# Attention outputs on array quarters, kv products on column halves, and identity transposes in TensorE's waits

## The chip, the core and the metric

The kernel runs on one core of a Trainium2 chip. It is one launch; the metric is the device time of that launch in microseconds (us). TensorE does the matmuls and the transposes, VectorE and ScalarE read its results from eight PSUM banks, GpSimd works on SBUF alone, and SyncE issues the loads and stores. The engines run side by side and wait for each other through counters (semaphores).

## What is computed

```python
# tok: (4, 512, 256, 4) image tensor to (4, 512, 256) tokens; joined with the 512 text tokens to x: (4, 1024, 256)
h = einsum('bhid,oi,od->bho', x, weighted_sum, weight)

# attention layer on the normalised x: 16 heads of 64, linear attention over 1024 tokens
q, k = elu(x @ Wq) + 1, elu(x @ Wk) + 1;  v = x @ Wv;  g = sigmoid(x @ Wg + bg)
kv = einsum('bhnd,bhne->bhde', k, v);  k_sum = k.sum(-2)
z = 1 / clip(einsum('bhnd,bhd->bhn', q, k_sum), 1e-6)
out = einsum('bhnd,bhde->bhne', q * 64**-0.5, kv) * z[..., None] * g
x = x + out @ Wo

# then twice, on (2, 2048, 256): windowed attention (8 heads of 64, window 128, rotary, one window back),
# and a feed-forward of hidden size 682 with a GELU gate behind a layer norm
```

## The kernel before

The phases follow each other, each in a block whose end all engines wait for: the image tokens (`tok_phase`), the linear attention (`attention_phase`), and for each of two layers the windowed attention (`local_phase`) and the feed-forward (`mlp_phase`). Products that need more than one pass of precision are three matmuls on split operands (`matmul3`, lines 117 to 119; a record each). A plain float32 matmul leaves two records in the trace, a transpose (a matmul against the identity) one.

**Attention.** A batch has 1024 tokens, 8 tiles of 128. First the keys of all tiles are made and multiplied with the normalised x (`g_products`), which gives a matrix of 256 x 1024 in banks 2 to 5. ScalarE copies it out in four pieces (`take_g`, L516), and `kv_products` multiplies it with Wv (`attn_wv`, which carries one more column for the sum of the keys). Heads go in pairs: one matmul of a 128x128 stationary block with 129 moving columns makes the kv blocks of two heads, of which only the two diagonal 64x64 blocks are wanted; VectorE copies those, and the two key sums, out of banks 4, 5 and 3 into `kv`, whose other blocks are zero (`take_kv`, 12 copies, L660 and L661). The 4 stages u of a batch take two tiles each: queries (`queries`, four parts f), gates (`gates`, two halves a tile), head outputs (`outputs`), and, one stage later, the output transposes and products with Wo (`out_transposes`, `out_products`) and the residual.

`outputs` multiplies a pair's q (128 channels x 128 tokens, stationary) with its 128x130 block of `kv`: 128 columns of outputs and two of denominators. A tile's eight pairs go in groups of 3, 3 and 2, which use banks 4 and 5 in turn. VectorE answers each group in `gated` with four operations: the clipped denominator (L641), its reciprocal (L643), the multiply (L645) and the gate (L649). A bank is free when the group's fourth operation is done. TensorE's order is written out in `batch`: between the groups of a stage stand gate halves, each six matmuls of 512 columns, and the output products.

**Local attention.** `step(n, ...)` on each engine handles tile n's projections (banks 0 and 1), the turn of q and k and the scores of tile n-1, and probabilities and values of tile n-2. The turn (`turned_t`) waits for GpSimd's rotated q and k (L1075), the scores use array quarters already: 64 rows and 64 columns of the array each, with 64, 128 or 192 moving columns (L1391); the values use column halves (L1415). Four steps at the head and three at the end are written out, the others loop.

**Feed-forward.** `group` works on four tiles; its first group's normalised input is transposed at the end of the local phase (L1492).

SyncE issues all loads in one queue in the order of the code: in the first phase the image tiles (L192), between them the attention weights (L197).

## Time and profile before

| | us |
|---|---|
| median of 3 runs (lowest, highest) | 1915.9 (1913.65, 1916.27) |
| the profiled execution | 1916.24 |
| its span, first to last instruction | 1914.2 |
| TensorE busy in the span | 1841.3 (96%) |
| VectorE busy | 1512.0 (79%) |
| ScalarE busy | 1102.2 (58%) |
| GpSimd busy | 432.2 (23%) |
| image tokens | 0 to 62 |
| attention | 62 to 634 |
| local attention and feed-forward, layer 0 | 634 to 1068, 1068 to 1273 |
| layer 1 | 1273 to 1706, 1706 to 1914 |

The page gives for each engine the time in which at least one instruction ran. A matmul's record lasts longer than the array is taken by it (they are pipelined), so the pace is read from one start to the next. The granted clock is a share of 2.4 GHz: 1.00 is the higher of TensorE's two levels, 0.50 (1.2 GHz) the lower. Its mean over the span is 0.986.

### The profile page before, as it was taken

The numbers are of one execution on the slowest core, as the hardware profiler recorded it, in microseconds if no ns is written. First come the engines' busy times: TensorE is split into PE (matmuls) and PEld (weight loads), VectorE is DVE, ScalarE is ACT, GpSimd is POOL, SyncE is SP. The second block draws the span as 40 slices with busy tenths as digits, with TensorE's granted clock in tenths as the row PEclk, the third lists the DMA queues.
The fourth block names the chain that finished last, engine by engine and source line by source line (L and its number), as shares of the span: only waits on it lengthen the run. The fifth ranks groups of instructions, "written<-read, shape, count | busy, mean of one in ns | idle before, by whom it ended". The sixth has DMA issues, their size and how long they took to land. (4 is left out here: it accounts for less than half of the span.)

```text
span 1914.2 us, 44588 instructions
## 1 busy us (share of the span) xinstructions
PE 1841.3 (96%) x15388; PEld 1612.0 (84%) x15388; DVE 1512.0 (79%) x4715; ACT 1102.2 (58%) x2551; POOL 432.2 (23%) x319
## 2 busy tenths in 40 slices
PE   8899999999999799999999899989999999989998
PEld 8789889889889588888888788867888888868887
DVE  6888878878778688888888677768888888877777
ACT  4433433433433388888888444437888888853333
POOL 0000000000000244454444000014554545411111
PEclk9999999999999799999999999998999999999999
DMA  9100000000010100000000200010000000000002
GB/s 344 49 1 1 1 1 1 1 1 1 1 69 1 51 6 5 5 4 5 5 5 11 87 12 11 11 45 4 6 4 5 5 5 5 4 23 12 11 11 93
DMA packets 44983, 44.51 MB, mean 23 GB/s; under 512 B 8359, under 2 KB 39387, under 8 KB 44894
## 3 DMA queue, kind: packets, MB, share of 16 engines
q1 hardware_dynamic: 44894, 43.33, 6.9%
q8 instruction: 55, 0.90, 0.2%
q14 instruction: 34, 0.28, 0.0%
HBM read 34.93 MB, written 8.39 MB: 23 GB/s over the span
## 5 line engine op out<-in xcount | busy, mean ns | idle before, releaser
L1117 ACT ACTIVATE l_probs<-l_probs,l_negmax 128x256 f32<-128x256 f32 x512 | 253.1, 496 | 83.3 <-DVE l_negmax L1227 83.3
L1075 POOL TENSOR_TENSOR l_t<-l_t,l_rnorm 128x512 f32<-128x512 f32 x128 | 131.0, 1044 | 295.3 <-DVE l_rnorm L1244 295.3
L1070 POOL TENSOR_TENSOR l_t<-l_t,l_t 128x1024 f32<-128x1024 f32 x64 | 153.2, 2393 | 129.0 <-DVE l_t L1279 129.0
L117 PE MATMUL ps<-local_w_hi,l_xT 128*128 128x512 f32 x384 | 167.7, 437 | 9.0 <-DVE l_t L1279 3.3
L118 PE MATMUL ps<-local_w_lo,l_xT 128*128 128x512 f32 x384 | 153.7, 400 | 0.0
L486 ACT ACTIVATE attn_exp<-ps 128x512 f32<-128x512 f32 x128 | 76.4, 599 | 133.2 <-PE ps L119 133.2
L119 PE MATMUL ps<-local_w_hi,l_xT 128*128 128x512 f32 x384 | 153.1, 399 | 0.0
L1405 PE MATMUL ps<-ident,l_probs 128*128 128x128 f32 x1024 | 145.7, 279 | 1.6 <-ACT l_probs L1117 1.4
L117 PE MATMUL ps<-m_hnT_hi,ffn_w_hi 128*128 128x512 f32 (+1 forms) x352 | 142.4, 405 | 4.3 <-PEq L1017 4.3
L118 PE MATMUL ps<-m_hnT_lo,ffn_w_hi 128*128 128x512 f32 (+1 forms) x352 | 139.6, 396 | 0.0
L119 PE MATMUL ps<-m_hnT_hi,ffn_w_lo 128*128 128x512 f32 (+1 forms) x352 | 139.6, 396 | 0.0
L1123 ACT ACTIVATE l_probsT<-ps 128x512 f32<-128x512 f32 x256 | 134.3, 648 | 0.0
L1050 POOL MEMSET l_xT<- 128x520 f32 x2 | 1.1, 531 | 571.7 <-POOLq L450 569.8
L1405 PEld LDWEIGHTS ps<-ident,l_probs 128*128 128x128 f32 x1024 | 113.4, 140 | 17.5 <-issue 12.4
L1415 PE MATMUL ps<-l_probsT,l_v 128*64 128x128 f32 x2048 | 125.9, 276 | 0.7 <-DVE x L1195 0.7
L1415 PEld LDWEIGHTS ps<-l_probsT,l_v 128*64 128x64 f32 x2048 | 110.5, 137 | 12.1 <-issue 10.0
L1622 ACT ACTIVATE m_gelu<-ps,ffn_b 128x512 f32<-128x512 f32 x80 | 55.1, 688 | 109.5 <-PE ps L119 109.5
L1274 DVE TENSOR_TENSOR l_t<-ps,rope_c 128x1024 f32<-128x1024 f32 x64 | 78.4, 1225 | 40.7 <-PE ps L1399 38.9
L117 PE MATMUL ps<-attn_w_hi,attn_xT_hi 128*128 128x512 f32 x256 | 106.1, 414 | 3.8 <-PEq L185 2.1
L1609 ACT ACTIVATE m_u_hi<-m_u 128x512 fp32r<-128x512 f32 x80 | 50.5, 632 | 99.1 <-DVE m_u L1683 99.1
L1227 DVE CUSTOM_DVE_ANT_0 l_probs<-ps,mask_even 128x256 f32<-128x256 f32 x256 | 107.0, 419 | 0.0
L1227 DVE CUSTOM_DVE_ANT_0 l_probs<-ps,mask_odd 128x256 f32<-128x256 f32 x256 | 106.5, 419 | 0.1
(252 smaller groups left out, 5774.5 us busy)
## 6 DMA issues: line engine op xcount, KB each, us to landing
tok_x<-x SPq DMA_DIRECT2D x16, 512.0 KB, 7.9
m_shifted<-shifted SPq DMA_DIRECT2D x20, 256.0 KB, 2.8
shifted<-x SPq DMA_DIRECT2D x64, 64.0 KB, 1.5
out<-x SPq DMA_DIRECT2D x8, 512.0 KB, 4.2
ffn_w_raw<-ffn_w SPq DMA_DIRECT2D x6, 640.0 KB
local_w_raw<-ffn_wqkv SPq DMA_DIRECT2D x4, 768.0 KB, 5.6
tok_base<-attn_base SPq DMA_DIRECT2D x4, 512.0 KB, 8.6
h<-txt SPq DMA_DIRECT2D x4, 512.0 KB, 8.4
```

The source lines that it names most:

```text
L117: nc.tensor.matmul(out, wh, mh, start=start, stop=False, skip_group_check=True)
L118: nc.tensor.matmul(out, wh, ml, start=False, stop=False, skip_group_check=True)
L119: return nc.tensor.matmul(out, wl, mh, start=False, stop=stop, skip_group_check=True)
L486: nc.scalar.activation(ex[:, at % 2], ps[:, at % 2], ACT.Exp).then_inc(s.attn_exp.sem, 1)
L1070: nc.gpsimd.tensor_tensor(t1[:], t1[:], t2[:], ALU.add).then_inc(s.summed.sem, 1)
L1075: nc.gpsimd.tensor_tensor(v, v, rn[:, a * LH:(a + 1) * LH].unsqueeze(2).to_broadcast([P, LH, DH]), ALU.mult).then_inc(s.rotated.sem, 1)
L1117: last = nc.scalar.activation(v, v, ACT.Exp, bias=nb[:, h:h + 1], scale=-1.0, accum_out=rsum[:, h:h + 1])
L1123: nc.scalar.activation(pt[:, pair], ps[:, PT[pair]], ACT.Copy).then_inc(s.p_done.sem, 1)
L1227: last = nc.vector.tensor_tensor_reduce(pm[:, pair, e * 2 * P:(e + 1) * 2 * P], ps[:, bank, at:at + 2 * P], mask[:], -8.0, -LOWEST, ALU.ad ...
L1274: nc.vector.tensor_tensor(t1[:].rearrange("p a (h d) -> p a h d", d=DH), q, cw, ALU.mult)
L1405: last = nc.tensor.transpose(ps[:, PT[pair], k * P:(k + 1) * P], pm[:, pair, k * P:(k + 1) * P], K.ident[:])
L1415: last = nc.tensor.matmul(ps[e * DH:(e + 1) * DH, OT, pair * P:(pair + 1) * P], vv[:, w, h * DH:(h + 1) * DH], pt[:, pair, (2 * e + w) * P ...
```

## The change

**Outputs.** Each of the eight pairs of a tile now takes four matmuls: for each half of the tokens and each head of the pair, 64 rows by 64 columns of the array with 65 moving columns (64 outputs and the denominator). Head e writes bank 4 + e. `kv` has no zero blocks any more. A tile's pairs go in two groups of four, and each group uses both banks; a bank is free when the group's multiply, now counted by itself, is done. The second group of a stage's second tile is gated one stage later.

**kv products.** Each head has its own matmul per half of the contraction: 128 rows by 64 columns of the array, 65 moving columns. The first four pairs wait for the first two pieces of `take_g`, the others for all four. `take_kv` is two copies of 128x260. `attn_wv` is laid out in 16 blocks of 65 columns, so its loads go in rows of 64 elements.

**Transposes of the identity.** `keep_warm` issues `count` transposes of the identity into a bank; nobody reads them. They stand at the end of the image tokens (8), of the attention (10), at several places of each local phase (4, 10, 6, 20, 18, 8 around its first steps, 20, 8, 8 in its last three, 8 behind them), at each feed-forward's start (8) and after the first feed-forward (10).

```diff
+def keep_warm(nc, K, bank, count):
+
+    for _ in range(count):
+        nc.tensor.transpose(K.ps[:, bank, 0:P], K.ident[:], K.ident[:])
...
-    VC = P + 1
-    OC = P + 2
-    GROUPS = ((0, 3), (3, 6), (6, 8))
-    KV_BANKS = (4, 5, 3)
+    OC = DH + 1
+    PG = PAIRS // 2
...
             def gated(b, n, *groups):
                 for g in groups:
...
+                    done = OB * b + 4 * n + 2 * g
+                    dve.wait_ge(*s.attn_o_full.after(FB * b + 2 * n + g + 1))
+                    out = ps[:, 4:6, 0:PG * OC].rearrange("p e (m c) -> p m e c", c=OC)
+                    heads = (lambda v: v.rearrange("p (m e) -> p m e", e=2).unsqueeze(3))
+
+                    chain(nc.vector.tensor_scalar(heads(zd[:]), out[:, :, :, DH:OC], 1e-6, 2.0 * DH ** 0.5, ALU.max, ALU.mult))
+                    chain(nc.vector.reciprocal(z[:], zd[:]))
+                    nc.vector.tensor_tensor(o1[:, g].rearrange("p (m e d) -> p m e d", e=2, d=DH), out[:, :, :, 0:DH],
+                                            heads(z[:]).to_broadcast([P, PG, 2, DH]), ALU.mult).then_inc(s.attn_o.sem, 1)
+                    dve.wait_ge(*s.attn_o.after(done + 1))
...
             def take_kv(b):
...
+                for g in range(2):
+                    done = nc.vector.tensor_copy(kv[:, g * PG:(g + 1) * PG, :],
+                                                 ps[:, 4 + g, 0:PG * OC].rearrange("p (m c) -> p m c", c=OC))
...
             def kv_products(b):
-                pe.wait_ge(*s.attn_gt.after(4 * b + 4))
...
+                for g in range(2):
+                    pe.wait_ge(*s.attn_gt.after(4 * b + 2 * g + 2))
+                    for m in range(g * PG, (g + 1) * PG):
                         for c in range(KC):
...
+                            for e in range(2):
+                                h = 2 * m + e
+                                last = nc.tensor.matmul(ps[e * DH:(e + 1) * DH, 4 + g, m % PG * OC:(m % PG + 1) * OC],
+                                                        gt[:, c, h * DH:(h + 1) * DH], wv[:, c, h, :],
+                                                        start=(c == 0), stop=(c == KC - 1))
...
+            def outputs(b, u, which, g):
                 n = 2 * u + which
...
+                pe.wait_ge(*s.attn_o.after(OB * b + 4 * n + 2 * g - 1))
+                for m in range(g * PG, (g + 1) * PG):
+                    for half in range(2):
+                        tokens = slice(half * DH, (half + 1) * DH)
+                        for e in range(2):
+                            r = slice(e * DH, (e + 1) * DH)
+                            last = nc.tensor.matmul(ps[tokens, 4 + e, m % PG * OC:(m % PG + 1) * OC],
+                                                    qt[r, m, which * P + half * DH:which * P + (half + 1) * DH], kv[r, m, :],
+                                                    start=True, stop=True)
+                last.then_inc(s.attn_o_full.sem, 1)
...
                 if b:
                     wait(pe, s.masked, 4 * (n - 1))
+                    if second:
+                        keep_warm(nc, K, OT, 20)
+                    if drain(n, 0):
+                        wait(pe, s.turned, n)
+                        keep_warm(nc, K, QK, 20)
                     turned_t(n - 1, 0)
...
+                if second:
+                    keep_warm(nc, K, OT, 18)
                 if b:
                     wait(pe, s.qk_done, 2 * n)
...
+            keep_warm(nc, K, OT, 4)
             x_t(0, 0)
+            keep_warm(nc, K, OT, 10)
             schedule(pe, step)
+            keep_warm(nc, K, V, 8)
...
+            keep_warm(nc, K, 4, 8)
             group(0, 0, False)
...
-            ("attn_wv", [P, KC, PAIRS, P + 1], F32),
+            ("attn_wv", [P, KC, 2 * PAIRS, DH + 1], F32),
```

TensorE, first stage of the first batch, around the first tile's head outputs (L848 before, L853 now; the rows between are a gate half). Before:

```order
L848 MATMUL ps<-attn_kv,attn_qT 128x130 x6
L117 MATMUL ps<-attn_w_hi,attn_xT_hi 128x512
L118 MATMUL ps<-attn_w_lo,attn_xT_hi 128x512
L119 MATMUL ps<-attn_w_hi,attn_xT_lo 128x512
L117 MATMUL ps<-attn_w_hi,attn_xT_hi 128x512
L118 MATMUL ps<-attn_w_lo,attn_xT_hi 128x512
L119 MATMUL ps<-attn_w_hi,attn_xT_lo 128x512
L848 MATMUL ps<-attn_kv,attn_qT 128x130 x2
```

Now:

```order
L853 MATMUL ps<-attn_kv,attn_qT 64x65 x16
L117 MATMUL ps<-attn_w_hi,attn_xT_hi 128x512
L118 MATMUL ps<-attn_w_lo,attn_xT_hi 128x512
L119 MATMUL ps<-attn_w_hi,attn_xT_lo 128x512
L117 MATMUL ps<-attn_w_hi,attn_xT_hi 128x512
L118 MATMUL ps<-attn_w_lo,attn_xT_hi 128x512
L119 MATMUL ps<-attn_w_hi,attn_xT_lo 128x512
L853 MATMUL ps<-attn_kv,attn_qT 64x65 x16
```

Six matmuls, then two, on both sides of the gate half have become sixteen and sixteen.

VectorE at the same place, its answer to the outputs, behind the last operation of the norm (L133, now L139). Before:

```order
L133 SCALAR_TENSOR_TENSOR attn_rstd<-attn_tmp,attn_rstd 128x8
L641 TENSOR_SCALAR attn_den<-ps 128x6
L643 RECIPROCAL attn_z<-attn_den 128x6
L645 TENSOR_TENSOR attn_o_1032<-ps,attn_z 128x384
L649 SCALAR_TENSOR_TENSOR attn_out<-attn_tanh,attn_o_1032 128x384
L641 TENSOR_SCALAR attn_den<-ps 128x6
```

Now:

```order
L139 SCALAR_TENSOR_TENSOR attn_rstd<-attn_tmp,attn_rstd 128x8
L646 TENSOR_SCALAR attn_den<-ps 128x8
L647 RECIPROCAL attn_z<-attn_den 128x8
L648 TENSOR_TENSOR attn_o_1040<-ps,attn_z 128x512
L654 SCALAR_TENSOR_TENSOR attn_out<-attn_tanh,attn_o_1040 128x512
L646 TENSOR_SCALAR attn_den<-ps 128x8
```

The operations are the same four; they cover 512 elements instead of 384, and a tile has two such groups instead of three.

TensorE in the second step of a local phase, from the last projection to the scores (L1403 is the turn of q and k, L1370 the turn of the next x, L1395 the scores). Before:

```order
L119 MATMUL ps<-local_w_hi,l_xT 128x512
L1399 MATMUL ps<-ident,l_t_8239 128x128 x8
L1366 MATMUL ps<-ident,l_x 128x128 x2
L1391 MATMUL ps<-l_kT,l_qT 64x128 x4
```

Now:

```order
L119 MATMUL ps<-local_w_hi,l_xT 128x512
L125 MATMUL ps<-ident 128x128 x20
L1403 MATMUL ps<-ident,l_t_8728 128x128 x8
L1370 MATMUL ps<-ident,l_x 128x128 x2
L125 MATMUL ps<-ident 128x128 x18
L1395 MATMUL ps<-l_kT,l_qT 64x128 x4
```

Twenty transposes of the identity stand ahead of the turn, eighteen ahead of the scores.

## Rows read from the trace of the kernel before

**Rows 1.** Windows: us; busy (instructions) per engine, PEclk (granted clock), DMA share, GB/s

```profile
62.00:620.60 558.60, 549.63 (x3588) 495.28 (x3588) 441.29 (x1093) 216.92 (x402) 1.09 (x2) 1.00 0.02 7
637.00:676.00 39.00, 30.52 (x229) 23.99 (x230) 29.73 (x109) 19.60 (x52) 12.83 (x9) 0.79 0.19 58
```

**Rows 2.** Timeline of TensorE, one stage's outputs: start, us, engine, line, operands, count

```profile
192.97 1.51 PE L848 MATMUL ps<-attn_kv,attn_qT 128*128 128x130 f32 x12
194.23 0.47 PE L117 MATMUL ps<-attn_w_hi,attn_xT_hi 128*128 128x512 f32 x1
...
201.04 0.83 PE L848 MATMUL ps<-attn_kv,attn_qT 128*128 128x130 f32 x6
```

**Rows 3.** Timeline of TensorE, local scores (array quarters) and values (column halves), from several windows

```profile
683.03 0.27 PE L1424 MATMUL ps<-ident,l_spread 128*128 128x128 f32 x1
683.23 0.51 PE L1391 MATMUL ps<-l_kT,l_qT 64*64 64x128 f32 x12
683.23 0.56 PE L1391 MATMUL ps<-l_kT,l_qT 64*64 64x128 f32 x16
683.23 1.57 PE L1391 MATMUL ps<-l_kT,l_qT 64*64 64x128 f32 x64
684.73 1.97 PE L1415 MATMUL ps<-l_probsT,l_v 128*64 128x128 f32 x32
```

**Rows 4.** Timeline of VectorE in a stage: a 512-element feature, denominator, multiply

```profile
188.66 0.69 DVE L598 SCALAR_TENSOR_TENSOR attn_qT<-ps,attn_exp 128x512 f32<-128x512 f32 x1
...
193.84 0.17 DVE L641 TENSOR_SCALAR attn_den<-ps 128x6 f32<-128x6 f32 x1 [0.46 <-PE ps L848]
...
194.27 0.56 DVE L645 TENSOR_TENSOR attn_o<-ps,attn_z 128x384 f32<-128x384 f32 x1
```

**Rows 5.** Timelines of ScalarE and TensorE around kv; group of VectorE's larger copies

```profile
255.91 2.06 ACT L516 ACTIVATE attn_out<-ps 128x512 f32<-128x512 f32 x4 [2.15 <-PE ps L119]
258.02 3.84 PE L823 MATMUL ps<-attn_wv,attn_out 128*128 128x129 f32 x32 [0.72 <-ACT attn_out L516]
261.62 0.36 PE L117 MATMUL ps<-attn_xT_hi,attn_w_hi 128*128 128x256 f32 x1
L660 DVE COPY attn_kv<-ps 64x192 f32<-64x192 f32 (+1 forms) x24 | 8.0, 333 | 2.4 <-PE ps L823 2.1
```

**Rows 6.** Timeline of TensorE, end of attention and second and third local step

```profile
622.90 1.94 PE L947 MATMUL ps<-ident,attn_out 128*128 128x128 f32 x8 [2.24 <-DVE attn_oT_lo L759]
...
650.99 2.12 PE L1399 MATMUL ps<-ident,l_t 128*128 128x128 f32 x8 [2.75 <-POOL l_t L1075]
...
661.48 0.63 PE L118 MATMUL ps<-local_w_lo,l_xT 128*128 128x512 f32 x1
661.91 0.63 PE L119 MATMUL ps<-local_w_hi,l_xT 128*128 128x512 f32 x1
...
664.42 0.60 PE L1399 MATMUL ps<-ident,l_t 128*128 128x128 f32 x4
```

**Rows 7.** Timeline of TensorE, start of layer 0's feed-forward

```profile
1068.77 0.47 PE L117 MATMUL ps<-m_hnT_hi,ffn_w_hi 128*128 128x512 f32 x1 [2.14 <-PEq L1017]
...
1073.64 0.39 PE L119 MATMUL ps<-m_hnT_hi,ffn_w_lo 128*128 128x512 f32 x1
1073.87 0.40 PE L117 MATMUL ps<-m_hnT_hi,ffn_w_hi 128*128 128x512 f32 x1
```

**Rows 8.** Timelines of GpSimd and TensorE, first step of layer 0's drain

```profile
1042.97 2.04 POOL L1075 TENSOR_TENSOR l_t<-l_t,l_rnorm 128x512 f32<-128x512 f32 x2 [4.72 <-DVE l_rnorm L1244]
1044.16 0.63 PE L1399 MATMUL ps<-ident,l_t 128*128 128x128 f32 x4 [2.59 <-POOL l_t L1075]
```

**Rows 9.** Window of TensorE with transposes alone: busy (records), granted clock, DMA

```profile
1042.60:1046.10 3.50, 1.94 (x17) 1.00 0.01 2
```

**Rows 10.** Timeline of SyncE's issues in the first phase

```profile
15.43 3.27 SPq L197 DMA_DIRECT2D attn_wv<-attn_Wv  x2
...
26.48 0.93 SPq L197 DMA_DIRECT2D attn_w_raw<-attn_Wq  x2
```

More of the change, by code:

```diff
@@ L838, in queries @@
                 last.then_inc(s.attn_a_full.sem, 1)
-            def outputs(b, u, which, *groups):
+            def outputs(b, u, which, g):
                 n = 2 * u + which
@@ L843, in outputs @@
                 pe.wait_ge(*s.attn_kv.after(b + 1))
-                for g in groups:
-                    m0, m1 = GROUPS[g]
-                    pe.wait_ge(*s.attn_o.room(OB * b + 3 * n + g, 2))
-                    for m in range(m0, m1):
-                        last = nc.tensor.matmul(ps[:, 4 + (3 * n + g) % 2, (m - m0) * OC:(m - m0 + 1) * OC],
-                                                qt[:, m, which * P:(which + 1) * P], kv[:, m, :],
-                                                start=True, stop=True)
-                    last.then_inc(s.attn_o_full.sem, 1)
+                pe.wait_ge(*s.attn_o.after(OB * b + 4 * n + 2 * g - 1))
[8 more added lines that the diff above has]
+                last.then_inc(s.attn_o_full.sem, 1)
             def out_transposes(b, last, u, which):
```

84 lines of the change are left out of this document (36 added, 48 removed).

## The prediction

> **What bounds the kernel now.** I read first the stages by windows, then the timelines of TensorE and of the engines that it waits for. In the attention stage TensorE is busy 549.6 of 558.6 us and VectorE 441.3 [rows 1]: what is taken off TensorE there comes off the time, as long as VectorE's answers come in time. At the head of each local layer the picture is another: in 39 us TensorE works 30.5, at a mean granted clock of 0.79 [rows 1]. There a chain over ScalarE, VectorE and GpSimd sets the pace, and TensorE stands at the lower of its two levels (1.2 GHz) for part of its work. The profiled execution took 1916.2 us, its span is 1914.2; the median of the runs is 1915.9, so the sum is made against 1916.2 and needs no shift worth naming.
>
> **Head outputs.** Before, 16 records of 130 columns make a tile (two per matmul): 12 of them from 192.97 to 194.23, 0.105 each, and six in 0.83 us, of which the last takes 0.28, 0.11 each [rows 2]. That is some 3.46 us for the 32 records of a stage (two tiles). Now 64 records of 65 columns make a tile, on four array quarters in turn. The trace has that form in the local scores. Going from 12 to 16 records, four records of 64 columns, lengthens the run by 0.05 us [rows 3], and the whole run, half of it fours of 128 columns, takes 64 records from 683.23 to 684.73 [rows 3]. I take 0.055 for a four: eight fours are 0.44. Around a group the array changes its form: 683.03 to 683.23 is 0.20 where such records stand 0.11 apart, and the step out costs as much again, so a group is 0.44 + 0.2 = 0.64, say 0.66. Four groups are 2.64, 0.82 less per stage. Twelve stages (three of each of four batches) give **9.8 us**; the fourth is in the batch heads below. Bounds: without the change of form 0.46 a group, 13 us more for 64 groups; with fours at twice 0.055, 28 us less.
>
> **Can VectorE keep up?** The two output banks now hold one group at a time: the next group waits for the multiply of the one before. Behind that wait stand, in TensorE's order, everything else of the stage. A group's answer is tensor_scalar, reciprocal and multiply. From 193.84 the multiply begins 0.43 later; over 512 elements it takes about 0.69, as the 512-element feature does [rows 4]. With the hand-over that is 1.25 us; between the two groups lie the six projections of a gate half, 6 x 0.23 = 1.4 (the two records of this form at the higher level, [rows 7]). It fits, by a tenth. The other pairs are parted by the same, by 12 projections of 256 columns, or by 2.8 us of output products. I count no wait in a stage. VectorE's own work falls too (two groups of four operations a tile instead of three), which keeps it from becoming late in its turn; the late group, now half a tile, delays the next features by 0.6, which nobody waits for.
>
> **Batch heads.** The kv products take 258.02 to 261.62 and stand 0.72 idle before, for the last of ScalarE's four copies, 2.06 us together [rows 5]. Now half of them need two copies only, so that idle goes. 64 records of 65 columns on column halves come in pairs; the 128-column pairs of the values take 32 records in 1.97 us [rows 3], so I take half of it for a pair, 0.057, and 2.0 for all. TensorE is 2.3 us ahead. VectorE takes kv over in two copies (0.85) instead of 12, whose larger six are 8.0 us in 24 records over four batches [rows 5], with the small ones 2.5 a batch. Behind them stand two features and ten small operations before the first gate, so VectorE, 2.2 ahead, now makes TensorE wait some 0.5 for the first multiply. With 0.8 for the outputs of the stage a head gives 2.9; in the first batch VectorE is held by the subtraction for Wo's low part ahead of it, and I take 2.3. Sum **11.0 us**. If column halves do not overlap at 65 columns, 6 of these are lost.
>
> **End of attention.** TensorE waits 2.24 us for VectorE there [rows 6]; one group of four operations in place of two saves 0.9 of the chain. The clock was low right after: the eight transposes took (1.94 - 0.35) / 7 = 0.23 each, twice 0.11, and the 20 products behind them, half as wide as those of [rows 7], lose some 0.1 each. About 2.4 of that lies on the path. The wait is now shorter, and whether the clock falls again I leave even: 1.2. Together **2.1**.
>
> **The turned identity.** 264 transposes are added, 118 for each layer with its feed-forward start. One is one record of 128 columns, 0.11 us; 29 us in all, of which what fits in a wait is free. What they bring is clock, and only where TensorE is on the chain. Step by step through layer 0: 10 behind the last product (1.1 us) lie beside two sums and statistics of VectorE; 4 and 10 lie in the waits around the first turn. 20 (2.2 us) fit in the 2.75 before 650.99 [rows 6]; 18 end before the scores. At the higher level the turn of q and k ends 0.4 earlier (its second half waits for GpSimd), and the 12 projections from 659.64, nine of them at 0.43 each, end 2.4 us earlier (0.43 from one start to the next at the lower level, 0.23 at the higher, [rows 6, 7]), but then GpSimd's rotated halves are the later ones, which gives 1.0 at 664.42 [rows 6]; of all that I keep 0.9 beside 0.4 from the first projections, since VectorE has its late statistics to finish. **1.3** for layer 0. Layer 1 has no late statistics: its first projections, at the lower level too, would go from 0.43 to 0.23, and 1.4 us pass through; **2.4**. Feed-forward start: eight transposes stand ahead of the first product, 0.9 lost, since the first product, at 1068.77, waits only for the barrier; eight products behind it, at the lower level, go from 0.43 to 0.23, 1.6 won [rows 7]. **1.4** for two. Drain: 20 transposes begin only when the last mask is done, just before GpSimd begins at 1042.97, so they end at about 1045.0, while q's half was turned from 1044.16 [rows 8]. That is a delay of 0.85 on a chain in which all wait, twice: **minus 1.7**. The rest (8 each) fits.
>
> Do transposes hold the clock? From 1042.6 to 1046.1 TensorE did nothing but transposes, busy 1.94 of 3.5 us, and the granted clock stayed 1.00 [rows 9]. The page "TensorE: Matmul & The Clock Gate" of the Trainium skill, in Part 4 (PE-mode transpose), says that the full clock does not engage for transposes, which don't count as busy the same way; by it the added work would buy nothing. The row speaks against it, though for holding a clock, not for raising it.
>
> **Loads.** Wv lands in chunks of 64 elements instead of 128. Issuing its two halves took SyncE 3.27 us where Wq, in long rows, took 0.93 [rows 10], and image tiles queue behind it on SyncE while the first stage waits for them. Bounds 0 (queues absorb it) and 2.3 (as much again); near the lower, as the following issue waits for room anyway: **minus 0.7**.
>
> **Sum.** 9.8 + 11.0 + 2.1 + 1.3 + 2.4 + 1.4 - 1.7 - 0.7 = 25.6: 1916.2 - 25.6 = **1890.6 us**.
>
> **Rivals.** *The warm work doesn't hold the clock.* The ramps then stay at 1.2 GHz and a transpose costs about twice 0.11, as those at 622.90 did [rows 6]: 20 would end 1.7 after their wait, 18 and the next 8 some 3 later. No gain of 6.3, and about 3 lost in each layer: 1890.6 + 6.3 + 6 = 1903. For it: the transposes at 650.99 ran at the lower level and did not raise it. Against it: [rows 9]. Chance 0.12. *Output banks.* If the chain to the multiply takes 0.5 more than I add up, two of four groups a stage wait, 16 us in all: 1907. Chance 0.06. *Column halves don't overlap* in the kv products: 1897, chance 0.08. *Cheap quarters*: no cost for the change of form, and all cold stretches gone: 13 + 3 less, 1875; with half of it 1882; chance 0.1. *Slower:* only two of the four quarters run at once, as the column halves of the values do. Then a record is 0.03 us (half of 1.97 / 32), a group 0.96 + 0.2 = 1.16, 64 groups cost 32 us more: 1923. It turns slower once a group costs 0.40 more than my 0.66. What speaks against it is the 0.05 for four. Chance 0.03. The same page, in Part 1, gives a floor of about 25 ns from one start to the next however few the columns; by it a group of 32 would be 1.0 us and the time about 1912. Four records more in 0.05 us [rows 3] speak against it. Chance 0.01.
>
> **How the numbers follow.** The forecast case has 0.6. Its own range is 1884 to 1897. The range for 8 in 10 takes in the kv case and the clock case: 1881 to 1904; outside stay the bank case, the two-quarter case and the floor, and half of the cheap case. A measurement of this kernel tells about 0.2% (4 us) from no change. Faster by more needs under 1912: 0.94; within 0.02; slower 0.04.
>
> **What would show it.** Groups of 32 records of 64x65 in about 0.66 us from start to next, with no idle before them but once a batch; kv in 2.0 us without the 0.72 before it; attention from 558.6 to about 538; a granted clock of 1.00 from 637 on in the local ramps, and 0.85 more before the turn in the drain. Wrong would be: idle before most output groups, released by the multiply (bank case); groups over 1 us; a clock at 0.5 under the added transposes; a later end of the first stage, released by image tiles.

## The result, and the profile after the change

The changed kernel took **1905.3 us** (median of four runs, 1903.2 to 1906.5) beside 1916.1 of the kernel before on the same chip: a ratio of 0.9947, 95% interval 0.9934 to 0.9960. It is faster, by 10.8 us or 0.5%. The forecast was 1890.6 with a range of 1881 to 1904, so the time lies outside, and less than half of the forecast gain came. The profiled execution of the changed kernel took 1904.3 us, 12.0 less than that of before; the ledger below is made against these two.

The windows of the changed kernel, with the columns of [rows 1]:

```profile
62.00:620.00 558.00, 549.11 (x5306) 474.70 (x5305) 424.06 (x937) 218.54 (x404) 0.21 (x1) 1.00 0.03 7
620.00:637.00 17.00, 13.27 (x73) 10.88 (x72) 9.82 (x31) 3.87 (x7) 3.90 (x7) 0.84 0.47 142
637.00:676.00 39.00, 35.34 (x392) 30.09 (x392) 29.64 (x109) 25.32 (x66) 15.99 (x12) 0.98 0.01 3
627.00:666.00 39.00, 32.18 (x279) 26.70 (x278) 29.61 (x109) 19.56 (x52) 12.82 (x9) 0.91 0.18 56
```

Against [rows 1]: in 637 to 676 the granted clock is 0.98 instead of 0.79. But the same work now stands some 10 us earlier, and in 627 to 666 the clock is 0.91; that is the figure to set beside 0.79. The attention stage is where the forecast and the trace part. TensorE's last products of attention come 11 us earlier, not 22.

**A ledger by the same record.** Both timelines hold the same fp32 products in the same order, only other records stand between them. So the start of one product before and after says how far the changed kernel is ahead at that place. Each line is one such record, starts in us. Within a stage the lead swings by some 0.5, since the old first group holds three pairs and the new one four, so batches are compared at the same place of a stage: the last product ahead of a stage's first group. The head of a batch is all that lies up to its second stage's outputs, the kv products and the first stage's outputs with it.

```
place                              before    after    ahead
end of the first stage              64.09    65.01    -0.93
batch 0, at stage 2's outputs      147.51   146.69     0.82
batch 0, behind its stages         246.09   244.79     1.30
batch 1, at stage 2's outputs      286.80   283.17     3.63
batch 1, behind its stages         386.94   382.88     4.06
batch 2, at stage 2's outputs      426.05   419.67     6.38
batch 2, behind its stages         528.70   521.87     6.83
batch 3, at stage 2's outputs      565.71   556.67     9.04
batch 3, at stage 4's outputs      610.13   600.95     9.18
last output product's run          630.41   619.43    10.98
layer 0, first turn                650.99   642.41     8.58
layer 0, third step                671.23   661.12    10.11
layer 0, before the drain         1040.09  1029.96    10.13
layer 0, in the drain             1046.80  1037.47     9.33
feed-forward start, layer 0       1075.04  1064.83    10.21
layer 1, first product            1275.12  1265.12    10.00
layer 1, third step               1315.16  1302.89    12.27
layer 1, in the drain             1694.80  1683.43    11.37
feed-forward start, layer 1       1716.85  1704.59    12.26
last transposes' end              1906.39  1894.46    11.93
```

The heads give 1.8, 2.3, 2.3 and 2.2, together 8.6. The stages behind them give 0.5, 0.4, 0.5 and 0.1, together 1.5 for eleven stages, 0.14 each, where 0.82 was forecast; the twelfth stands with the end of attention. That end gives 1.8, layer 0's ramp loses 0.9, layer 1's gives 2.3, each drain loses 0.8 and each feed-forward start gives 0.9 at first.

**A group of head outputs** in the changed kernel's timeline of TensorE, with the product ahead of it and the ones behind:

```profile
193.63 0.40 PE L118 MATMUL ps<-attn_w_lo,attn_xT_hi 128*128 128x512 f32 x1
193.87 0.39 PE L119 MATMUL ps<-attn_w_hi,attn_xT_lo 128*128 128x512 f32 x1
194.19 0.70 PE L853 MATMUL ps<-attn_kv,attn_qT 64*64 64x65 f32 x32
194.81 0.50 PE L117 MATMUL ps<-attn_w_hi,attn_xT_hi 128*128 128x512 f32 x1
195.15 0.39 PE L118 MATMUL ps<-attn_w_lo,attn_xT_hi 128*128 128x512 f32 x1
```

and the products ahead of the first record of [rows 2], before the change:

```profile
192.51 0.39 PE L118 MATMUL ps<-attn_w_lo,attn_xT_hi 128*128 128x512 f32 x1
192.74 0.40 PE L119 MATMUL ps<-attn_w_hi,attn_xT_lo 128*128 128x512 f32 x1
```

The group is 194.19 to 194.81, 0.62 (0.63 in the median of 54), where the forecast had 0.66. But the last product ahead of it holds TensorE from 193.87 to 194.19, 0.32; before, from 192.74 to 192.97, 0.23. And the first product behind it takes 0.34 to the next (194.81 to 195.15); that behind the old group, at 194.23, took 0.31. A part of the price of the form stands on its neighbours.

**kv and the rest of a head** (TensorE, batch 0):

```profile
117.37 2.09 PE L826 MATMUL ps<-attn_wv,attn_out 128*64 128x65 f32 x64
119.39 0.38 PE L117 MATMUL ps<-attn_xT_hi,attn_w_hi 128*128 128x256 f32 x1
...
124.42 0.47 PE L117 MATMUL ps<-attn_w_hi,attn_xT_hi 128*128 128x512 f32 x1 [1.90 <-issue]
```

2.02 for 64 records, where [rows 5] had 3.60 for 32, with no idle time ahead. In batch 0 TensorE then stands 1.90 before the first gate (1.29 before the change): it waits for kv, which VectorE takes over only behind the subtraction for Wo's low part. That 0.6 is lost again there.

**End of attention and layer 0's ramp**, windows (same columns) and timelines of TensorE and VectorE:

```profile
611.23:614.64 3.41, 1.19 (x9) 0.84 (x8) 2.53 (x5) 1.79 (x4) 0.00 (x0) 1.00 0.00 0
614.64:618.05 3.41, 3.02 (x14) 3.05 (x15) 1.50 (x4) 0.05 (x1) 0.00 (x0) 0.50 0.00 0
628.29:631.71 3.42, 1.06 (x5) 0.53 (x3) 2.87 (x17) 2.09 (x4) 0.00 (x0) 1.00 0.96 362
631.71:638.53 6.82, 5.96 (x17) 4.89 (x18) 6.52 (x15) 0.00 (x0) 2.36 (x1) 0.50 0.44 124
```

```profile
612.90 1.16 PE L950 MATMUL ps<-ident,attn_out 128*128 128x128 f32 x8 [1.64 <-DVE attn_oT_lo L760]
...
628.27 0.17 DVE L157 TENSOR_REDUCE l_rstd<-h_stats 128x8 f32<-128x16 f32 x1 [2.25 <-DMA mask_odd<-mask_prev]
...
632.57 0.80 PE L117 MATMUL ps<-local_w_hi,l_xT 128*128 128x512 f32 x1 [3.21 <-DVE l_xT L1191]
```

The wait at the end of attention is 1.64 instead of 2.24 [rows 6], and the clock still falls behind it, in 614.64 to 618.05, after a stretch in which TensorE worked 1.19 of 3.41 us. Then something that the forecast didn't have: VectorE's late statistics wait 2.25 for the masks' DMA, which they don't read. TensorE stands idle for 3.21, until the l_xT that VectorE makes behind the statistics is there, and the clock falls for the 6.8 us in which it has to catch up. The masks landed late too, from the table of DMA issues (last column: us from issue to landing; 1.8 before):

```profile
mask_odd<-mask_prev SPq DMA_DIRECT2D x1, 64.0 KB, 3.0
```

**Drain, feed-forward start, loads** (GpSimd, TensorE, SyncE's issues), which answer to [rows 8], [rows 7] and [rows 10]:

```profile
1032.84 2.05 POOL L1079 TENSOR_TENSOR l_t<-l_t,l_rnorm 128x512 f32<-128x512 f32 x2 [4.72 <-DVE l_rnorm L1248]
...
1032.71 2.37 PE L125 MATMUL ps<-ident 128*128 128x128 f32 x20 [1.28 <-issue]
1034.92 0.49 PE L1403 MATMUL ps<-ident,l_t 128*128 128x128 f32 x3
...
1059.31 1.06 PE L125 MATMUL ps<-ident 128*128 128x128 f32 x8 [1.12 <-PEq L1021]
1060.12 0.48 PE L117 MATMUL ps<-m_hnT_hi,ffn_w_hi 128*128 128x512 f32 x1
...
15.56 7.44 SPq L203 DMA_DIRECT2D attn_wv<-attn_Wv  x2
```

From the start of the rotation to the first turned record it is 2.08 (1032.84 to 1034.92) where it was 1.19 in [rows 8]: 0.89 for the 20 transposes. The two issues for Wv take SyncE 7.44 instead of 3.27.

### The profile page after: what moved, and what is told of

Read it like the earlier page. It is cut to its first block and busy times, and to the rows that moved or that the text cites. A ratio compares the mean times of both kernels' runs of the same rounds, so it can differ in the third digit from the quotient of the medians.

```text
span 1902.2 us, 48258 instructions
## 1 busy us (share of the span) xinstructions
PE 1848.1 (97%) x17316; PEld 1601.8 (84%) x17316; DVE 1488.2 (78%) x4547; ACT 1102.7 (58%) x2551; POOL 431.6 (23%) x318
## 5 line engine op out<-in xcount | busy, mean ns | idle before, releaser
L117 PE MATMUL ps<-local_w_hi,l_xT 128*128 128x512 f32 x384 | 165.7, 432 | 6.4 <-DVE l_xT L1191 3.2
L119 PE MATMUL ps<-local_w_hi,l_xT 128*128 128x512 f32 x384 | 151.3, 394 | 0.0
L117 PE MATMUL ps<-m_hnT_hi,ffn_w_hi 128*128 128x512 f32 (+1 forms) x352 | 141.0, 401 | 0.0
L119 PE MATMUL ps<-m_hnT_hi,ffn_w_lo 128*128 128x512 f32 (+1 forms) x352 | 138.3, 393 | 0.0
L117 PE MATMUL ps<-attn_w_hi,attn_xT_hi 128*128 128x512 f32 x256 | 106.8, 417 | 3.5 <-issue 1.9
```

Source lines behind the costliest of these rows:

```text
L117: nc.tensor.matmul(out, wh, mh, start=start, stop=False, skip_group_check=True)
L119: return nc.tensor.matmul(out, wl, mh, start=False, stop=stop, skip_group_check=True)
```

## The experiments

The theory after reading the trace (A): the quarters cost as forecast inside a group, and give most of the gain back on the records around it and through a shift of Wo in memory; ramps and drains are, but for layer 0's ramp, nearly as forecast. Its rivals: the added transposes eat the gain; or the outputs are worth what was forecast, and it is lost elsewhere. The changed kernel is the starting point of each unless said.

### Which half of the change brings what

**forms_only**: `keep_warm` issues nothing, and the drain's wait ahead of it is gone.

> The changed kernel without any of its added transposes: head outputs on quarters and kv on column halves stay. Theory A (the trace of the changed kernel read by TensorE's starts): the groups of 32 records take 0.63 us, as forecast, but the projection ahead of a group takes 0.32 instead of 0.23 and the step out of a group 0.15 instead of 0.03, so the stages gain nothing like 0.82 each; attention is worth 11 us less 1 for the loads, and the added transposes bring next to nothing in sum: 1905 to 1907. Theory B (the prediction's sum): the forms are worth 22 us and the transposes lose most of it again: 1894.

1909.1 us (ratio 0.9963, 0.9951 to 0.9975): 7.1 better than before. That is 2 above A's range, and B's 1894 is out. What A missed is in its trace: the first stage ended 2.6 late instead of 0.9, and in batch 0's head, behind the idle 1.9 us, the clock fell:

```profile
126.00:129.40 3.40, 3.31 (x8) 2.61 (x9) 3.12 (x11) 0.55 (x1) 0.00 (x0) 0.55 0.00 0
```

In the profile of the changed kernel the same products ran at 1.00 behind the same idle time. The difference is 1.6 us; what decides over it isn't shown.

This run also shows the clock rising under transposes. In the first drain step TensorE has only the kernel's own transposes (of q and k, and of the probabilities) from 1037.32 to 1041.56; in the first window below it is busy throughout at 0.50, and from its end on the clock is 1.00:

```profile
1037.72:1041.13 3.41, 3.41 (x19) 3.41 (x17) 3.24 (x13) 1.94 (x5) 1.90 (x2) 0.50 0.00 0
1041.13:1044.54 3.41, 3.41 (x25) 3.15 (x24) 2.54 (x16) 1.71 (x4) 0.00 (x0) 1.00 0.00 0
```

**warm_only**: the kernel before with the transposes.

> The kernel before with all of the added transposes and nothing else of the change. Theory A: layer 1's ramp gains 2.4, the two drains lose 0.8 each and the two feed-forward starts gain 0.7 each, layer 0's ramp, where TensorE only comes to the late statistics' wait earlier and stands idle longer, gives between -0.9 and +0.5: 1912.5 to 1915. Theory B: if the transposes are what lost the gain, 1925 or more.

1912.3 (0.9980, 0.9971 to 0.9988): 3.8 better than before. With forms_only the two make 10.9, the whole change 10.8: they add. By the ledger it gains 0.3 in layer 0's ramp, 2.2 in layer 1's, and next to nothing over a drain and the feed-forward start behind it. The profiled execution (1914.1) is only 2.1 better than that of before; it is the second slowest of twelve. The transposes did not lose the gain.

**kv_halves_only**: head outputs as before.

```diff
-                            last = nc.tensor.matmul(ps[tokens, 4 + e, m % PG * OC:(m % PG + 1) * OC],
...
+                        last = nc.tensor.matmul(ps[:, 4 + (3 * n + g) % 2, (m - m0) * OC:(m - m0 + 1) * OC],
+                                                qt[:, m, which * P:(which + 1) * P], kv[:, m, :],
```

> The changed kernel with its kv products on column halves and its added transposes, but with the head outputs as before (full array, two heads a record of 130 columns, groups of 3, 3 and 2 pairs, kv block-diagonal and filled by four copies). Theory A: quarters are worth nothing in the stages, only about 1 at the end of attention; 1905 to 1908, level with the changed kernel within 2. Theory B: quarters are worth 0.82 in each of 16 stages and the loss is elsewhere: 1918.

1913.7 (0.9988, 0.9979 to 0.9997). Between the two: the quarters are worth 8.4, neither 0 nor 13. Theory A was wrong in saying that they bring nothing in the stages: beside the kernel before, this kernel **loses** 0.6 to 0.9 us in every three stages although its outputs are the old ones. So a part of the loss in the stages is not the quarters'. It stands on the products with Wo: 24 records of L117 to L119, in the timelines of before (the first two rows), of the changed kernel (the next two) the first and the last of one such run:

```profile
442.51 0.28 PE L117 MATMUL ps<-attn_wo_hi,attn_oT_hi 128*128 128x256 f32 x1
...
445.14 0.28 PE L119 MATMUL ps<-attn_wo_hi,attn_oT_lo 128*128 128x256 f32 x1
```

```profile
435.86 0.28 PE L117 MATMUL ps<-attn_wo_hi,attn_oT_hi 128*128 128x256 f32 x1
...
438.61 0.28 PE L119 MATMUL ps<-attn_wo_hi,attn_oT_lo 128*128 128x256 f32 x1
```

2.63 from first to last before, 2.75 after. Over the runs of the attention stage they are 2.62, 2.79 or 2.72 before (11, 11 and 6 of them) and 2.76 or 2.86 after (17 and 11): 2.71 and 2.80 on average.

### What the form costs, and whose

**row_halves**: one record for 128 tokens on each row half, 16 in place of 32.

```diff
-                    for half in range(2):
-                        tokens = slice(half * DH, (half + 1) * DH)
...
+                        last = nc.tensor.matmul(ps[:, 4 + e, m % PG * OC:(m % PG + 1) * OC],
+                                                qt[r, m, which * P:(which + 1) * P], kv[r, m, :], start=True, stop=True)
```

> The changed kernel with its head outputs on two row halves instead of four quarters: 16 records of 65 columns a group, each for 128 tokens, in place of 32. Same banks, same waits, same order. Theory A1: the price stands on the change between fp32 projections at full array and a divided array, whatever the division: entry 0.32, exit 0.15, inside 0.47 as before; 1905 within 1.5. Theory A2: the price goes with the columns' division, and with the tokens whole the entry is 0.23 and the exit 0.03: 64 groups by 0.2, 1892. Theory C: two row halves don't run at once, then a pair costs 0.11 and a group 0.4 more: 1931.

1928.1 (1.0061, 1.0047 to 1.0074; the median of six, of which one took 5052 us; without that one it is 1927.7), some 22 slower than with quarters:

```profile
202.25 0.40 PE L119 MATMUL ps<-attn_w_hi,attn_xT_lo 128*128 128x512 f32 x1
202.57 1.11 PE L851 MATMUL ps<-attn_kv,attn_qT 64*128 64x65 f32 x16
203.61 0.39 PE L117 MATMUL ps<-attn_wo_hi,attn_oT_hi 128*128 128x256 f32 x1
```

Two answers. The step in is 0.32 again (202.25 to 202.57): A1 holds for a division by rows alone as for quarters. Column halves pay it too: in the changed kernel the product ahead of kv takes 0.21 (255.72 to 255.93), where its like stand 0.12 apart.

```profile
255.72 0.28 PE L119 MATMUL ps<-attn_xT_hi,attn_w_lo 128*128 128x256 f32 x1
255.93 2.09 PE L826 MATMUL ps<-attn_wv,attn_out 128*64 128x65 f32 x64
```

So all three divisions of this kernel cost 0.09 on the record ahead. The second answer: the group is 1.04 for half the records, so the row halves do not run at once here, a record is some 0.06 by itself, as long as a four of quarters. That is C's mechanism, and 22 of its 26 us.

**groups_twice**: each group issued twice in a row, `for m in [*range(g * PG, (g + 1) * PG)] * 2`.

> The changed kernel with each group of head outputs issued twice in a row, 64 records in place of 32, the same result written again. Theory A (a four of quarters costs 0.0587 and the rest of a group's price, some 0.4 in all, is entering and leaving the form): 64 groups by 8 x 0.0587 = 0.47, 30 us more, 1935, and the group in the trace 1.10 from its first start to the next instruction. Theory B (the price is by the record, 0.9 for 32 with what stands on its neighbours): 64 x 0.9 = 58 us more, 1963.

1932.2 (1.0091, 1.0075 to 1.0106), some 27 more:

```profile
201.73 0.40 PE L119 MATMUL ps<-attn_w_hi,attn_xT_lo 128*128 128x512 f32 x1
202.06 1.16 PE L853 MATMUL ps<-attn_kv,attn_qT 64*64 64x65 f32 x64
203.15 0.50 PE L117 MATMUL ps<-attn_w_hi,attn_xT_hi 128*128 128x512 f32 x1
```

64 records take 1.09 where 32 took 0.63: 0.466 for eight fours, 0.058 each, and 64 groups of it are 30. By the ledger each stage of batch 1 loses 1.8, four times 0.466, but the head of the batch only 1.3: there a part of it lies in waits. The step in is the 0.32 or 0.33 of the single group. A holds: the rest of a group's cost, 0.16 inside the group's span and 0.11 on its neighbours, is paid per entry, however many records follow. The page "TensorEngine Tiling (Array Packing)" of the Trainium skill, under Key Properties, says that changing the tiling mode drains TensorE. No run shows the drain itself, but the rows show a price of that kind: 0.09 more ahead, the first four 0.11 where later ones stand 0.058 apart, and 0.15 from the last record to the next product, where the old group had 0.03.

### Wo's place

**wo_aligned**: 64 unused bytes a partition.

```diff
-            ("attn_wv", [P, KC, 2 * PAIRS, DH + 1], F32),
+            ("attn_wv", [P, KC, 2 * PAIRS, DH + 1], F32), ("attn_pad", [P, 16], F32),
```

> The changed kernel with 64 bytes of unused space a partition behind Wv, so that Wo's two parts lie 128 bytes from where they lay before the change instead of 64. In the trace of the kernel before, output products (attn_wo read as the moving side) start 116 ns apart on average, in that of the changed kernel 120, over some 660 records, and the same 120 stands where only kv was changed. Theory A: the place in memory makes that difference; 2.5 us less than the changed kernel, 1903. Theory B: it comes from what else reads and writes at that time; 0, 1905.

1902.3 (0.9923, 0.9909 to 0.9937), 3.0 better by the medians. By the ledger against the changed kernel it gains 0.2 to 0.5 in each batch, 1.5 in all, and the runs of 24 records are 2.71 and 2.81 instead of 2.76 and 2.86. So the place counts, with half the size that theory A gave it; the other half of the 3.0 isn't traced: in the profiled execution, 1.9 better in all, the clock did not fall at the end of attention (1.3 gained) and did in batch 0's head (1.6 lost). Why the place matters isn't shown. The 64 bytes move Wo on to 128 bytes behind its old place, not back to it, kv moves with it, and half of the difference to before is left (2.75 on average, beside 2.71 before and 2.80 in the changed kernel).

**full_outputs_aligned**: kv_halves_only with the same 64 bytes, which put Wo where it is in wo_aligned (its old place is 128 bytes in front of that).

> Head outputs as before on the full array, kv products on column halves, added transposes, and the 64 bytes behind Wv that put Wo back in its old place. Beside the changed kernel with the same 64 bytes (1902.3) it gives what the quarters alone are worth. By the prediction's sum 13 us for 64 groups and 0.9 at the end: 1916. By the trace (0.73 a stage inside the groups, less 0.35 for the entries and 0.1 for the first projection behind): 16 x 0.3 + 1.5 = 6 us: 1908.5.

1911.3 (0.9978, 0.9968 to 0.9987). Quarters alone are worth 1911.3 - 1902.3 = 9.0 by the medians: above the 6 from the trace, below the 13.9 of the forecast. But not all of that is the price of the groups. Beside wo_aligned, place by place: 3.4 in eleven stages, which is 0.3 a stage where 0.82 was forecast; 1.0 in each head, since with whole outputs VectorE fills kv by four copies and TensorE waits longer for it (2.88 in batch 0 and 0.63 in batch 1, where wo_aligned has 1.90 and nothing); 3.2 at the end of attention, where the clock fell in this profile and not in that of wo_aligned; and 1.0 lost again behind. In batch 3 its stages take what they took before: 47.995 us from the record at 550.34 on, 47.923 before.

### The other terms

**no_wait_gates**: `pe.wait_ge(*s.attn_kv.after(b + 1))` ahead of `gates(b, 0)` is left out.

> The changed kernel without the wait for kv ahead of the first gate of a batch (it was there since the kv products used gate bank 3, which they no longer do; the head outputs behind it keep theirs). Theory A: in the first batch TensorE stands idle 1.9 us there, of which the six projections that now move in front take most, until VectorE's features are the later ones: 1.0 to 1.9 less, and in some executions 1.6 more, where that gap makes the clock fall; 1903.5. Theory B: the features of VectorE are what ends the wait anyway and nothing moves: 1905.

1904.6 (0.9933, 0.9919 to 0.9946). In batch 0 the kernel is 2.0 ahead of its own earlier lag at the gate and has lost it again behind the second group of outputs. That is B: TensorE waits 1.21 for a feature and 0.87 for the multiply instead.

Its profile shows something else: the clock fell neither at the end of attention nor in the ramp (1.00 from 611 to 640, 0.82 there in the changed kernel), and it gained 2.4 there with the same code and nearly the same waits (1.64 and 3.31 idle, 1.64 and 3.21 in the changed kernel). What decides over such a fall isn't shown.

**drain_light**: no 20 transposes in the drain; the 8 at the feed-forward's start moved to the end of the local layer.

> The changed kernel without the 20 transposes ahead of the turn in the drain, and with the 8 ahead of the first feed-forward product moved to the end of the local layer (18 in place of 8 there). Theory A (each is in the path): 0.8 and 0.7 come back in each of two layers, the clock stays up: 3.0 less, 1902.3. Theory B: without the 8 at the start of the feed-forward the clock falls there as before the change and costs 1.6 each: 1.6 - 1.8 = no gain, 1905.5.

1905.5 (0.9939, 0.9925 to 0.9953), no difference. By the ledger the drain gains its 0.8 twice, as A has it. The 18 transposes at the layer's end cost 0.5, since the feed-forward starts only when TensorE is through them, and the 8 at the start had cost 0.7, so that moving them gains 0.1 in layer 0. In layer 1 the clock falls behind it, and of the lead 2.6 is lost, 1.6 of it on products at the lower level:

```profile
1712.96:1716.37 3.41, 3.41 (x10) 2.64 (x9) 2.73 (x5) 1.26 (x2) 0.00 (x0) 0.50 0.26 76
```

**ramp0**: 14 transposes in the last wait of attention, and the masks' wait behind the statistics.

```diff
+            keep_warm(nc, K, 0, 14)
             pe.wait_ge(*s.attn_o.after(OB * B))
...
-            if layer == 0:
-                dve.wait_ge(*s.const_in.after(16 * len(K.tables(0) + K.signs + K.masks)))
             late_stats()
+            if layer == 0:
+                dve.wait_ge(*s.const_in.after(16 * len(K.tables(0) + K.signs + K.masks)))
```

> The changed kernel with two edits around the end of attention: 14 transposes of the identity in the wait for the last head outputs, and VectorE's wait for the masks moved behind the late statistics, which don't read them. Theory A: the clock's fall there costs the last output products 1.3 us; the masks land 2.25 us after VectorE has nothing else to do, and TensorE's 3.6 us of idle behind the second projection, which makes the clock fall for the next 6.8 us, is mostly that wait: 1.3 + 2 to 3, 1901.5. Theory B: GpSimd's rotation is the later one in the ramp whatever is done before it, so that only the first edit counts: 1904.

1903.9 (0.9934, 0.9920 to 0.9947). By the ledger it is 1.3 ahead of the changed kernel behind the first edit and 4.4 behind both, at a clock of 1.00 throughout:

```profile
611.00:640.00 29.00, 25.26 (x176) 21.49 (x175) 17.61 (x52) 8.40 (x15) 6.25 (x9) 1.00 0.27 83
```

A, in the trace. Of the 4.4 the profiled execution keeps 2.3 (1901.9 beside 1904.3), since a fall of the clock at 1073 in the feed-forward took 1.9 back; the medians differ by 1.4.

**loads_split**: Wv's second half issued behind the next image tile.

> The changed kernel with Wv's two halves issued behind two image tiles instead of both behind one. In the traces of kernels with Wv in 64-element chunks the first stage ended 0.7 to 2.9 us later than before the change (mean 1.7 of eight), with Wv as before 0 and 0.3. Theory A: the two issues in a row (7.4 us of SyncE) are what the image tiles wait for, and split they fit between them: 1 to 1.7 less, 1904. Theory B: the transfers themselves, in four times as many small pieces, are what delays the tiles: no difference, 1905.3.

1906.0 (0.9947, 0.9934 to 0.9961). B: no difference, the first stage ended 3.5 late in its profile. Wv's two issues took SyncE 0.70 and 0.56 now, but the image tile between them 4.98. (A piece of 64 elements is half of the old one, so there are twice as many, not four times.)

**all_but_wo_lo** and **all_edits**: the padding, the ramp's edits, the drain without its 20, Wv's halves apart and 10 transposes in the first feed-forward group's wait; all_edits also moves the subtraction for Wo's low part behind `gated(b, 1, 0)`.

> The changed kernel with what the runs so far point to, together: Wo aligned as before (-2.5), no 20 transposes in the drain (-1.6), 14 transposes in the last wait of attention and the masks' wait behind the late statistics (-2.5 to -4), Wv's halves apart (-1), and 10 transposes in the first feed-forward group's wait for its normalised tile, where the clock fell in one of the runs. Theory A (the edits lie on different stretches and add): 1897. Theory B (one late arrival gives way to the next): 1901.

> The same, and in the first batch VectorE's subtraction for Wo's low part (2.29 us) is taken out of the way of kv and stands behind the first three groups of head outputs. Theory A: TensorE's 1.9 us of idle there goes, and with it the fall of the clock seen in two of the runs: 1.9 less than the kernel without this edit on average, 1895. Theory B: features and the outputs' multiply then are late by as much in the stage behind: no difference.

1899.4 (0.9913, 0.9900 to 0.9927) and 1897.7 (0.9910, 0.9895 to 0.9926). Not all of it adds: the first profile has falls of the clock in batch 0's head (1.5) and in the drain (1.5), where the 20 transposes no longer stand; in the drain it fell in wv_staged too, and not in all_edits or drain_light. Behind the moved subtraction TensorE gains 2.1 and loses 1.7 again, to features that are later by as much (waits of 0.49 and 1.14 at 136 and 139): B, but for the clock, which never falls in that profile while TensorE has work:

```profile
core 0: 1894.7 us, clock 0.999
```

**wv_staged**: Wv in long rows, where loads_split had only spread its pieces; its two issues stand together again.

```diff
-        K.attn_raw = [[(K.attn_wv[:, c, :, 0:DH], K.attn_wraw[:, k - (k > 1), c])[k != 1] for c in range(KC)]
+        (wv_raw,), _ = mem.place(K.attn_rest - PAIRS * D * 4, mem.norm, ("attn_wv_raw", [P, KC, INNER], F32))
+        K.attn_raw = [[(wv_raw[:, c], K.attn_wraw[:, k - (k > 1), c])[k != 1] for c in range(KC)] for k in range(4)]
...
+                out = K.attn_wv[:, c, :, 0:DH]
-            done = nc.vector.tensor_tensor(raw, raw, row, ALU.subtract)
+            done = nc.vector.tensor_tensor(out, raw, row, ALU.subtract)
```

> All edits of the best kernel so far, but Wv is loaded in its long rows (as Wq is) into the place that Wo's raw weights take later, and VectorE's subtraction of the base row, which ran in place, writes it into the layout of 64 elements and a gap. No instruction more. Theory A (the small pieces of Wv's transfer are what delays image tiles): the first stage ends 1 to 2.5 us earlier, 1896. Theory B (the tiles are late for another reason): no difference, 1897.7.

**1894.9** (0.9895, 0.9880 to 0.9911), the best kernel of the study, 20.4 below the kernel before (1915.3 beside it) and 10.4 below the changed one. SyncE issues both halves in 0.91:

```profile
16.46 0.91 SPq L203 DMA_DIRECT2D attn_wv_raw<-attn_Wv  x2
```

and its first stage ends with that of before (within 0.05 at 78 and 103 us). A: the small pieces were the loss, 2.8 us by the medians. With the pieces the first stage's delay was 0.8 to 3.5 us, by the kernel; one profile of each was taken.

## Why the prediction was wrong, step by step

- **Head outputs, 9.8 forecast, 1.5 in the ledger (0.14 a stage for 0.82). This is the step that failed.** It was "around a group the array changes its form, ... so a group is 0.44 + 0.2". The group itself came out as said: 0.058 for a four (0.055), 0.63 a group (0.66). What stands around it was left out. All starts of TensorE from 275.40 to 376.06 (before), the last three stages of batch 1 and the products behind them, summed by what stands ahead and what follows, give in us:

```
                                        before   after
inside the groups (81, 372 steps)         9.08    5.76    -3.32
step into a group (12)                    2.46    3.52    +1.06
step out of a group (12)                  0.66    1.76    +1.10
transposes of normalised x, and out (16)  1.59    1.51    -0.08
product to product (489)                 78.52   79.89    +1.37
all                                                       +0.13
```

  The first row and the third are what the sum priced: 9.74 before and 7.52 after, 0.74 a stage for the forecast 0.82 (the old base was counted 0.2 too high, as 0.11 for each of 32 records, while the last of each group holds TensorE only 0.03). The second row, 0.35 a stage, stands on the products ahead: the sum looked only from a group's first start on. Of the last row 0.25 is the first product behind a group, 0.41 a wait for a feature that still belongs to the head (without it the three stages gain 0.28), 0.49 goes with the 64 bytes (79.40 in wo_aligned), and 0.22 is spread over many products. The groups by themselves, Wo's place being equal, are worth 0.3 a stage (full_outputs_aligned). A change of form was seen in [rows 3], from full array to quarters, and its 0.20 used as the whole price; but the two other places where it shows, the record ahead and the product behind, were never looked at there.
- **Batch heads, 11.0 forecast, 8.6.** kv is right: 2.02 (2.0) and without its idle 0.72, which puts TensorE 2.4 ahead in batch 1 (2.3). But the sum has a slip: 2.3 - 0.5 + 0.8 is 2.6, not 2.9, so its own terms give 10.1. The outputs of the first stage failed as the others did: in batch 1 they gain 0.5 and not 0.8. The feared wait of 0.5 came as one of 0.4 in each batch, for a feature behind these outputs and not for the multiply, and some 0.1 goes with Wo's place. Batch 0 gave 1.8 for 2.3, since its wait for kv grew by 0.6.
- **VectorE keeps up: right.** TensorE's waits in the attention stage name the multiply once, 0.4 us. The rival of the banks is out, as is that of the column halves.
- **End of attention, 2.1 forecast, 1.8.** The clock fell again in this profile, behind 1.64 us of waiting. With 14 transposes in the wait it falls in none of four profiles (ramp0 is one), without them in nine of twelve. The 1.8 has the last stage's outputs in it, so the 2.1 came in part only.
- **Layer 0's ramp, 1.3 forecast, -0.9.** The second step that failed: "of all that I keep 0.9 ..., since VectorE has its late statistics to finish". The statistics were named and what they wait for wasn't. They begin when the masks have landed, 3.0 us after the issue here and 1.8 before; TensorE comes to the wait sooner and stands longer: behind 3.0 to 3.6 us of idle the clock fell in eight of nine profiles, behind the 0.9 of the four kernels that moved the wait in none. With it moved the ramp gains 2.1 (ramp0).
- **Layer 1's ramp, 2.4 forecast, 2.3. Feed-forward starts, 1.4 forecast, 1.8 at first, and 0.2 to 0.3 of each lost again later in the layer. Drains, -1.7 forecast, -1.7.** The first and the last are as worked out.
- **Loads, -0.7 forecast, -0.9 in this profile**, but 0.8 to 3.5 us lost over the kernels with the small pieces (wv_staged shows them to be the cause).
- **Do transposes hold the clock? Yes.** Layer 1's ramp shows it, before (first row), and so does the changed kernel, where the clock is 1.00 from 638.53 to the end of TensorE's work (second row):

```profile
1288.46:1302.11 13.65, 9.65 (x84) 7.97 (x85) 9.27 (x35) 7.21 (x21) 5.17 (x5) 0.50 0.00 1
638.53:1894.00 1255.47, 1228.80 (x11501) 1063.27 (x11501) 1005.76 (x3491) 850.48 (x2096) 424.45 (x304) 1.00 0.05 15
```

  They raise it too, as the rows of forms_only show. The page "TensorE: Matmul & The Clock Gate" of the Trainium skill, in Part 4, says that the full clock does not engage for transposes; the fp32 transposes of these traces have it otherwise, and the measurement decides. But the added transposes alone are worth 3.8 us (warm_only), in layer 1's ramp above all.
- The sum, with the terms as measured, is -0.9 + 8.6 + 1.5 + 1.8 - 0.9 + 2.3 - 1.7 + 1.3 = 12.0, the difference of the two profiled executions. The medians differ by 10.8; this profile is one with an early end of the first stage.
- The **range** failed for the same reason. The bounds of a group's price (0.46, twice 0.055) were put on what happens inside it; no case had a price outside. The rivals that come near in number did not happen: the clock case (1903), as the clock held, and the bank case (1907), as the multiply was waited for once. The one with a higher price for a group is the floor of about 25 ns a start (1912), which the page "TensorE: Matmul & The Clock Gate" of the Trainium skill gives in Part 1. It is out: it has a group at 1.0 us, and starts within a four stand 7 ns apart.

## What to carry to other kernels

A change of array form is priced from the start of the record ahead of the first divided one to the second product behind the last, against the same stretch in the old form: about 0.27 us here for each entry, so divided records pay when many follow one entry (0.058 for four of 65 columns), and hardly for 32 at a time between fp32 products: with Wo's place equal they gained 0.3 in a stage of four groups. When a wait is filled with work for the clock, look at the wait behind it too: TensorE comes to it sooner and may stand longer. Here that was a wait for a DMA that its waiter didn't need. Transfers that must land in pieces are better landed whole, when an operation that runs anyway can spread them.

## What the hardware showed that was not expected

- Two row halves (64 rows, 128 columns of the array, 65 columns moving) don't overlap: 16 records in 1.04 us, 0.056 each after the entry, about as much as a four of 64x64 quarters (0.058).
- The products with Wo change their pace with the place of the tensors in memory: 2.71 us on average for the same 24 records before, 2.80 in the changed kernel, 2.75 with 64 bytes more. Which address rule is behind it stays open.
- Whether the granted clock falls behind the same idle time changes from profile to profile. Behind 1.9 us of idle time in batch 0's head it fell in five profiles (forms_only, wo_aligned and all_but_wo_lo among them, at a cost of 1.5 or 1.6 us) and in four it did not, the changed kernel's being one; at the end of attention 1.19 busy of 3.41 us were followed by 0.50, and the same code kept 1.00 in no_wait_gates. Single profiles differ by 1 to 3 us for it, so small edits were judged by the ledger and not by medians alone.
- A 64 KB mask lands 1.7 to 2.2 us after its issue or 2.8 to 3.3: of the 64 transfers (four in each of 16 profiles) 49 are of the first kind and 15 of the second. The last of the four took 1.8 before the change and 3.0 in the changed kernel. What decides isn't shown.
